# Feed-forward weights staged in other buffers and made ternary in two passes, with new work orders

## What is computed

```python
x = x + tanh(g_xattn) * xattn(layernorm(x), ctx, mask)      # 8 heads of 64
x = x + tanh(g_ffn) * ffn(layernorm(x))                     # 512 -> 2048 -> 512

def act_quant(x):      # per row, 8 bits
    scale = 127.0 / clip(max(abs(x)), 1e-5)
    return clip(round(x * scale), -128, 127) / scale
def weight_quant(w):   # one scale for the whole matrix; values -1, 0, 1
    scale = 1.0 / clip(mean(abs(w)), 1e-5)
    return clip(round(w * scale), -1, 1) / scale
def bitlinear(x, w, b):
    return act_quant(rmsnorm(x)) @ weight_quant(w).T + b
def ffn(x):
    return bitlinear(gelu(bitlinear(x, w1, b1)), w2, b2)
```

## Time and profile before

| | us |
|---|---|
| three runs, lowest / median / highest | 1079.02 / 1079.19 / 1079.51 |
| the profiled execution, its own time | 1082.41 |
| its span, first to last instruction | 1080.6 |
| TensorE busy | 1017.6 (94%) |
| ScalarE busy | 854.5 (79%) |
| VectorE busy | 816.6 (76%) |
| GpSimd busy | 770.4 (71%) |

### The profile page before, as it was taken

How to read it: one execution, slowest core, us unless ns; L and a number is a source line. 1 busy time by engine, 2 the same in 40 slices (tenths; PEclk the granted TensorE clock), 3 DMA queues, 4 the chain that set the end, 5 groups by cost and what they waited for, 6 DMA issues and landing times.

```text
span 1080.6 us, 24141 instructions
## 1 busy us (share of the span) xinstructions
PE 1017.6 (94%) x8516; PEld 599.7 (55%) x8516; DVE 816.6 (76%) x1769; ACT 854.5 (79%) x1465; POOL 770.4 (71%) x743
## 2 busy tenths in 40 slices
PE   2958999999999999999999999999999999999686
...
GB/s 294 165 215 166 187 146 175 134 171 150 167 154 132 170 164 167 150 169 171 141 163 119 167 182 148 163 158 165 140 165 140 166 176 148 166 119 145 142 64 98
DMA packets 480038, 170.79 MB, mean 158 GB/s; under 512 B 458288, under 2 KB 460080, under 8 KB 479536
## 3 DMA queue, kind: packets, MB, share of 16 engines
...
## 4 chain that ended last, share of the span: by engine, by line
PE 81%; ACT 6%; POOL 4%; issue 3%; DVE 3%; DMA 2%; SPq 0%; ACTq 0%; DVEq 0%; POOLq 0%
PE ps_g L602 44%; PE ps_s L632 11%; PE ps_g L706 9%; PE ps_g L659 9%; PE ps_g L695 7%; PE ps_g L647 2%; POOL p L1097 1%; POOL ctx L1108 1%; ACT prob L961 1%; ACT hq L1056 1%; ACT p L968 1%; ACT h_sb L1049 1%; DMA xr<-in_wk 1%; DMA pt<-p 1%; ACT L1049 0%
## 5 line engine op out<-in xcount | busy, mean ns | idle before, releaser
L1097 POOL TENSOR_TENSOR p<-prob,p 112x750 f16<-112x750 f32 x256 | 402.6, 1580 | 118.2 <-ACT p L968 115.4
L782 DVE CUSTOM_DVE_ANT_0 prob<-ps_s,mbias 112x750 f32<-112x750 f32 x256 | 237.0, 936 | 93.3 <-PE ps_s L632 88.8
L602 PE MATMUL ps_g<-ctx,wk 128*128 128x375 f16 x1152 | 203.8, 328 | 34.9 <-POOL ctx L1108 31.2
L961 ACT ACTIVATE prob<-prob,rmin 112x750 f32<-112x750 f32 x256 | 233.0, 913 | 2.0 <-DVE rmin L782 1.6
L602 PE MATMUL ps_g<-wv,ctx 128*128 128x512 f16 (+1 forms) x864 | 199.5, 380 | 0.0
L602 PEld LDWEIGHTS ps_g<-ctx,wk 128*128 128x128 f16 x1152 | 111.2, 99 | 119.5 <-issue 30.0
L632 PE MATMUL ps_s<-k_sb,q_sb 64*112 64x375 f16 x1536 | 150.6, 329 | 7.1 <-DVE rmin L782 6.4
L602 PEld LDWEIGHTS ps_g<-wv,ctx 128*128 128x128 f16 (+1 forms) x864 | 85.1, 103 | 92.6 <-issue 6.3
L968 ACT ACTIVATE p<-prob 112x750 f16<-112x750 f32 x160 | 130.9, 821 | 7.0 <-DMA pt<-p 6.4
L632 PEld LDWEIGHTS ps_s<-k_sb,q_sb 64*112 64x112 f16 x1536 | 89.9, 127 | 63.8 <-issue 39.5
L659 PE MATMUL ps_g<-pt,v_sb 128*64 128x224 f16 (+1 forms) x2448 | 122.8, 255 | 1.5 <-DMA pt<-p 1.5
...
## 6 DMA issues: line engine op xcount, KB each, us to landing
...
pt<-p SPq DMA_TRANSPOSE x256, 4.0
...
```

The costliest lines, as they stand in the source:

```text
L602: mm = nc.tensor.matmul(out, lhs, rhs, start=(m == 0), stop=(m == len(steps) - 1))
L782: nc.vector.tensor_tensor_reduce(prob[:, (b * NU + n) % PROBS, :].rearrange("p (c k) -> p c k", c=2), ps_s[0:HT, n % 2, :, 0:CH], mbias[:, ...
L961: nc.scalar.activation(prob[:, (b * NU + n) % PROBS, :], prob[:, (b * NU + n) % PROBS, :], ACT.Exp, bias=rmin[:, n:n + 1], scale=-1.0, acc ...
L1097: nc.gpsimd.tensor_tensor(p16[:, u % HILO, 1, 0:J], prob[:, (b * NU + n) % PROBS, :], p16[:, u % HILO, 0, 0:J], ALU.subtract).then_inc(s[" ...
```

## The change

All in one file:
- The middle pass WR is gone, with its semaphore and its constant. WB now multiplies by the inverse mean and by 2^-9, in place. WQ cuts the float piece to between -2^-9 and 2^-9 and writes it as fp8, whose smallest step near zero is 2^-9, so that the conversion rounds to -2^-9, 0 or 2^-9. The factor is put right in the scales of the two products (one constant each).
- The pieces of both matrices are staged in w1's room, hq, hqt, xr, h_sb and b1, none in pt or v_sb. WA writes its unneeded output to a new small buffer. The waits of T:0:0 and V:0:1 on the weights go; the loads, LR and BD wait for WQ (w_quant) where they waited for WR.
- WM's first step, the sum over eight columns on VectorE, is a token of its own, WS.
- All five orders are new. The start reaches one batch further (FIRST is 2): pieces 8 to 15 are loaded, scaled and cut along with batch 1, and the first tile's feed-forward stands in the start. The cycle and the end hold the same work in another order.

```diff
-MAGIC = 12582912.0
+W_UNIT = 2.0 ** -9
-FIRST, LAST = 1, 14
+FIRST, LAST = 2, 14
 SP start
-    LX:0:0 PD:0:0 LC:0:0 LC:1:0 LC:2:0 PD:1:0 XT:0:0 LX:0:1 XT:1:0 LM:0:0 PD:2:0 WL:1:0 WL:0:0 WL:2:0 WL:3:0
-    WL:8:0 WL:4:0 WL:5:0 WL:6:0 WL:7:0 PD:3:0 WL:9:0 LC:0:1 LX:0:2 WL:13:0 LC:1:1 LC:2:1 WL:14:0 WL:12:0 WL:10:0
-    T:0:0 WL:11:0 T:1:0 T:2:0 T:3:0 WL:15:0 T:4:0 BD:0:0 T:5:0 XT:0:1 XT:1:1 T:6:0 T:7:0 T:8:0 LC:0:2 LC:1:2
...
+    LC:0:0 LX:0:0 PD:0:0 LC:1:0 LC:2:0 PD:1:0 PD:2:0 XT:0:0 XT:1:0 LM:0:0 WL:0:0 WL:1:0 WL:2:0 LX:0:1 LC:0:1
+    LC:1:1 WL:3:0 WL:4:0 WL:5:0 WL:6:0 WL:7:0 T:0:0 PD:3:0 LC:2:1 LX:0:2 T:1:0 LC:0:2 T:2:0 T:3:0 BD:0:0 XT:0:1
+    XT:1:1 T:4:0 T:5:0 T:6:0 LM:0:1 WL:8:0 WL:9:0 T:7:0 T:8:0 WL:10:0 WL:11:0 T:9:0 T:10:0 T:11:0 LR:1:0 LC:1:2
+    T:12:0 WL:12:0 T:13:0 T:14:0 WL:13:0 T:15:0 T:0:1 WL:14:0 WL:15:0 LC:2:2 XT:0:2 XT:1:2 T:1:1 T:2:1 T:3:1
...
 PE start
-    K:0:0 K:1:0 K:2:0 K:3:0 K:4:0 Q:0:0 Q:1:0 Q:2:0 S:0:0 V:0:0 V:1:0 V:2:0 K:5:0 K:6:0 S:1:0 K:7:0 S:2:0 WM:0:0
-    V:3:0 V:4:0 V:5:0 S:3:0 Q:3:0 K:0:1 K:1:1 S:4:0 V:0:1 V:1:1 S:5:0 V:2:1 V:3:1 S:6:0 WM:1:0 PV:0:0 K:2:1
...
+    K:0:0 K:1:0 K:2:0 K:3:0 K:4:0 Q:0:0 Q:1:0 Q:2:0 S:0:0 V:0:0 V:1:0 V:2:0 S:1:0 K:5:0 K:6:0 K:7:0 V:3:0 V:4:0
+    V:5:0 S:2:0 S:3:0 Q:3:0 WM:0:0 S:4:0 K:0:1 V:0:1 V:1:1 S:5:0 PV:0:0 V:2:1 V:3:1 S:6:0 K:1:1 K:2:1 K:3:1
...
 POOL start
-    N1:0:0 CX:0:0 CX:1:0 CX:2:0 N1:0:1 MB:0:0 L:0:0 L:1:0 WB:0:0 WB:1:0 WB:2:0 WB:3:0 H:2:0 CX:0:1 WB:4:0 WB:5:0
-    WB:6:0 WB:7:0 CX:1:1 CX:2:1 L:2:0 L:3:0 L:4:0 H:5:0 H:7:0 L:5:0 L:6:0 L:7:0 N1:0:2 L:8:0 WB:8:0 WB:9:0
...
+    CX:0:0 N1:0:0 CX:1:0 CX:2:0 MB:0:0 N1:0:1 L:0:0 L:1:0 H:2:0 L:2:0 L:3:0 CX:0:1 CX:1:1 L:4:0 CX:2:1 WB:0:0
+    WB:1:0 WB:2:0 H:5:0 L:5:0 L:6:0 WB:3:0 H:7:0 WB:4:0 N1:0:2 L:7:0 L:8:0 H:10:0 WB:5:0 PL:0:0 L:9:0 L:10:0
...
 PE cycle
-    S:5:0 PV:0:0 V:2:1 V:3:1 K:2:1 K:3:1 S:6:0 PV:1:0 K:4:1 F1:4:-1 F1:5:-1 F1:6:-1 F1:7:-1 S:7:0 V:4:1 F2:0:-1
-    K:5:1 S:0:1 PV:2:0 V:5:1 Q:2:1 S:1:1 K:6:1 K:7:1 S:2:1 F2:1:-1
+    PV:0:0 S:5:0 V:2:1 V:3:1 K:2:1 K:3:1 S:6:0 PV:1:0 K:4:1 F1:4:-1 F1:5:-1 F1:6:-1 F1:7:-1 S:7:0 V:4:1 K:5:1
+    S:0:1 V:5:1 F2:0:-1 PV:2:0 S:1:1 K:6:1 K:7:1 Q:2:1 S:2:1 F2:1:-1
 PE end, its last part
-    S:6:15 S:7:15 PV:3:15 F1:4:14 F1:5:14 F1:6:14 F1:7:14 PV:4:15 O:0:15 PV:5:15 PV:6:15 PV:7:15 O:1:15 F2:0:14
+    S:7:15 PV:2:15 PV:3:15 F1:4:14 F1:5:14 F1:6:14 F1:7:14 PV:4:15 PV:5:15 O:0:15 PV:6:15 PV:7:15 F2:0:14 O:1:15
     F1:0:15 F1:1:15 F1:2:15 F1:3:15 F1:4:15 F1:5:15 F1:6:15 F1:7:15 F2:1:14 F2:0:15 F2:1:15
...
+        rough = sb("rough", [128, WCH], BF16)
...
-        W2_AT = [halves_of_h[0], halves_of_h[1], halves_of_xr[0], halves_of_xr[1]] \
-            + [pt_words[:, n * WCH:(n + 1) * WCH] for n in range(3)] + [v_words[:, KC * D:KC * D + WCH]]
-        W1_AT = [own[0], own[1], halves_of_b1[0], halves_of_b1[1], halves_of_h[0], halves_of_h[1], halves_of_xr[0],
-                 halves_of_xr[1]]
+        in_hq = hq[:, :].bitcast(F32)
+        in_hqt = hqt[:, :, :].rearrange("p k q -> p (k q)").bitcast(F32)
+        W2_AT = [own[0], own[1], in_hq, in_hqt, halves_of_xr[0], halves_of_xr[1], halves_of_h[0], halves_of_h[1]]
+        W1_AT = [halves_of_b1[0], halves_of_b1[1], own[1], in_hq, in_hqt, halves_of_xr[1], halves_of_h[0],
+                 halves_of_h[1]]
         FLOATS = W2_AT + W1_AT
-        COMES_AFTER = {NW + 4: 0, NW + 5: 1, NW + 6: 2, NW + 7: 3}
-        COMES_LAST = (2 * NW - 2, 2 * NW - 1)
-        STAGED_IN = {0: 1, 1: 1, 2: 0, 3: 0, NW + 2: 3, NW + 3: 3}
+        COMES_AFTER = {NW + 2: 1, NW + 3: 2, NW + 4: 3, NW + 5: 5, NW + 6: 6, NW + 7: 7}
+        COMES_LAST = (4, NW + 5)
+        STAGED_IN = {4: 0, 5: 0, 6: 1, 7: 1, NW: 3, NW + 1: 3}
...
                     elif n in COMES_AFTER:
-                        sp.wait_ge(w_above, COMES_AFTER[n] + 1)
+                        sp.wait_ge(w_quant, COMES_AFTER[n] + 1)
...
                     u = b * NU + n
-                    if u == 0:
-                        sp.wait_ge(w_above, NW - 1)
...
                 if kind == "WQ":
-                    dve.wait_ge(w_above, n + 1)
-                    nc.vector.tensor_scalar(piece((w2, w1)[n // NW], n), above[n % 2], 2.0, -1.0, ALU.min, ALU.add,
-                                            saturate=False).then_inc(w_quant, 1)
+                    dve.wait_ge(w_near, n + 1)
+                    if n >= NW:
+                        dve.wait_ge(w_quant, NW + 3 if n >= NW + 4 else 2)
+                    nc.vector.tensor_scalar(piece((w2, w1)[n // NW], n), FLOATS[n], W_UNIT, -W_UNIT, ALU.min,
+                                            ALU.max, saturate=False).then_inc(w_quant, 1)
...
-                if kind == "WR":
-
-                    act.wait_ge(w_near, n + 1)
-                    if n >= 2:
-                        act.wait_ge(w_quant, n - 1)
-                    nc.scalar.activation(above[n % 2], FLOATS[n], ACT.Relu, bias=one_up[:, :]).then_inc(w_above, 1)
-                    return
...
                         act.wait_ge(wready, 3)
-                        act.wait_ge(w_above, NW)
...
-                    nc.gpsimd.tensor_scalar(FLOATS[n], FLOATS[n], winv[:, at:at + 1], MAGIC, ALU.mult, ALU.add)\
+                    nc.gpsimd.tensor_scalar(FLOATS[n], FLOATS[n], winv[:, at:at + 1], W_UNIT, ALU.mult, ALU.mult)\
                         .then_inc(w_near, 1)
```

More of the change, by code:

```diff
@@ new lines @@
+    F1:0:-1 F1:1:-1 F1:2:-1 F1:3:-1 N1:0:2 L3:1:-1 M:10:0 M:11:0 KL:1:1 PA:0:0 GM:0:-1 VL:2:1 G2:0:-1 VL:3:1
+    KL:2:1 KL:3:1 M:12:0 M:13:0 PA:1:0 KL:4:1 F1:4:-1 F1:5:-1 F1:6:-1 F1:7:-1 M:14:0 M:15:0 VL:4:1 GM:1:-1
+    G2:1:-1 M:0:1 M:1:1 XN:0:2 F2:0:-1 KL:5:1 VL:5:1 M:2:1 M:3:1 PA:2:0 M:4:1 XH:0:2 KL:6:1 M:5:1 KL:7:1 F2:1:-1
+    QL:2:1 PA:3:0 XH:1:2
+    """, """
+    M:6:14 QL:3:14 M:7:14 O:0:13 L2:0:13 M:8:14 L3:0:13 M:9:14 O:1:13 L2:1:13 VL:0:15 VL:1:15 KL:0:15 M:10:14
+    PA:0:14 KL:1:15 M:11:14 F1:0:13 F1:1:13 F1:2:13 F1:3:13 M:12:14 M:13:14 KL:2:15 KL:3:15 KL:4:15 L3:1:13
@@ L485, in build @@
         own = [w1[:, n * 4 * WCH:(n + 1) * 4 * WCH].bitcast(F32) for n in range(2)]
-        W2_AT = [halves_of_h[0], halves_of_h[1], halves_of_xr[0], halves_of_xr[1]] \
-            + [pt_words[:, n * WCH:(n + 1) * WCH] for n in range(3)] + [v_words[:, KC * D:KC * D + WCH]]
-        W1_AT = [own[0], own[1], halves_of_b1[0], halves_of_b1[1], halves_of_h[0], halves_of_h[1], halves_of_xr[0],
-                 halves_of_xr[1]]
-        FLOATS = W2_AT + W1_AT
-        COMES_AFTER = {NW + 4: 0, NW + 5: 1, NW + 6: 2, NW + 7: 3}
-        COMES_LAST = (2 * NW - 2, 2 * NW - 1)
-        STAGED_IN = {0: 1, 1: 1, 2: 0, 3: 0, NW + 2: 3, NW + 3: 3}
-        rough = [hqt[:, :, :].rearrange("p k q -> p (k q)").bitcast(BF16)[:, 0:WCH], xc[:, :].bitcast(BF16)]
-        above = [hq[:, :].bitcast(BF16)[:, n * WCH:(n + 1) * WCH] for n in range(2)]
+        in_hq = hq[:, :].bitcast(F32)
[3 more added lines that the diff above has]
+                 halves_of_h[1]]
+        FLOATS = W2_AT + W1_AT
+        COMES_AFTER = {NW + 2: 1, NW + 3: 2, NW + 4: 3, NW + 5: 5, NW + 6: 6, NW + 7: 7}
+        COMES_LAST = (4, NW + 5)
+        STAGED_IN = {4: 0, 5: 0, 6: 1, 7: 1, NW: 3, NW + 1: 3}
         def piece(w, n):
```

175 lines of the change are left out of this document (90 added, 85 removed).

## The result

The kernel after takes 1069.82 us as median of four runs (1066.89 to 1074.12), beside 1079.23 of the kernel before in the same series: 0.9913, interval 0.989 to 0.9937, so 9.4 us less. I had forecast 1060.2, 19 us less. The time lies in the stated range, near its upper end, and half of the forecast gain is missing. The same kernel was run twice more beside the experiments: 0.9922 (0.9907 to 0.9938) and 0.989 (0.9868 to 0.9911). The profiled execution has a span of 1072.3 us and took 1074.12, the longest of its four; against the span of before the gain to be explained is 8.3 us.

The account below looks back on a forecast made before the run. TensorE's own pace bounds the twelve batches, so time comes only from the ends. The start's 17.3 us, taken as 15, plus 4 at the end make 19: 1060.2 us off the median. Forecast 1056 to 1067, stated range 1051 to 1071.

Parts of the forecast that it names:

- First context: At the very start, the first context piece goes first, so the first matmul starts at 15.8 instead of 19.55: 3.7 us gained.
- Knot and waits: At 57 to 69 us, context ahead of weight pieces gains 5.8 us; shorter waits for q and attention low halves gain 3.8.
- Clock: In the start, TensorE's slow stretches after 69.29, 102.72 and 124.25 us all go: 4.0 us gained.
- Third pass: Weight rounding in the start: 18.2 us of ScalarE work goes, VectorE's clamping takes 1.9 us each; off the path.
- WL:15's cover: Near 100 us, this weight load holds up a context load, but batch 2's context has 10 us of cover.
- Twelve cycles: In the twelve batch cycles, the same products in another order: counted as zero.
- The 2 us of cover: In each cycle, turned hidden values take 10.3 us while TensorE has 12.3 us of other work: 2 us to spare.
- the twelvefold rival: Two transposes late in every cycle, the excess paid twelve times; slower, 1092 at 2.7 us excess; chance 0.06.
- The end: After the cycles, shorter row-minimum waits and earlier norm and quantization of tile 25: 4 us gained, bounds 0 and 8.
- row-minimum waits: At the end, two waits totalling 6.0 us shrink to about 2.0 each: gain 2.
- the slow run of 16 products: At the end, tile 25's feed-forward ran slow, 6.46 us, after waiting for turned input; its norm now comes before.
- VectorE as the bound of the start: Clamping passes all at 3.38 us add 32 us in the start and take back its gain: 1075 to 1079; chance 0.06.

Follow-up runs that it names:

- ctx_first: The kernel before with only the first context piece loaded, copied and split ahead of x and W_k; 1076.6 us, 0.9956.
- start_back: The kernel after with the start of the kernel before, keeping the new cycle and end; 1081.23 us, 1.0011.
- third_back: The kernel after with a ScalarE copy of each scaled weight piece added, for which VectorE's clamping waits; 1075.65 us, 0.996.
- knot_only: The kernel before with batch 1's context pieces moved ahead of weight pieces, keeping three passes and all buffers; 1081.9 us, 1.0.
- cycle_back: The kernel after with the cycle of the kernel before, keeping the new start and end; 1068.3 us, 0.9893.
- start_only: The kernel before with the start of the kernel after, keeping the old cycle and end; 1068.16 us, 0.989.

## Why half of the forecast gain is missing

- **First context, 3.7 forecast.** 4.0 in the profile (19.55 to 15.53), 4.4 in time by ctx_first. Right, and it passed through whole.
- **Knot and waits, 5.8 and 3.8 forecast.** From the first matmul to the first feed-forward product the waits sum to 19.2 us before (the earlier trace rows less the first, and two of 0.6 and 0.4) and 9.5 after: 9.7 against 9.6 (6.1 and 8.3 in the two repeats). The sum was right in this execution, its parts weren't: the context wait vanished altogether, q still cost 2.7, turned scores 1.9.
- **Clock, 4.0 forecast.** This step failed. I had counted all slow stretches as gone "since no wait after the first exceeds 3.1 us". None does, but behind the waits of 1.9, 1.9 and 2.7 stand products that take about 3.0, 1.6 and 1.4 us more than at full clock (51 to 58, 101 to 106, 120 to 123 us): 6.0. Before had 5.0 and not 4.0: the prediction left out twelve products at 104.69 us that take 2.45 us where the same take 1.32 elsewhere. For the same 914 products of the start TensorE is busy 114.6 us before and 115.5 after, so the term is minus 0.9 instead of 4.0, 4.9 us off, and the largest error of this execution. 4.0 + 9.7 - 0.9 is the 12.8 measured. In the two repeats the term is minus 1.2 and plus 2.3, under 4.0 in each. Before's own start was busy only 112.2 us in start_back's profile, so one pair of profiles gives this term to some 2 us.
- **Third pass, off the path.** The clamping pass has a mean of 1.2 us against 1.9 forecast, and the 16 keep VectorE busy 19.0 us where before had 22.4. But third_back says that ScalarE's pass was worth about 5 us: the prediction that it lies off the path was wrong. Whether ScalarE's load or the extra handover counts isn't shown. I had the gain in the knot's row without giving it its cause; knot_only shows that the order of GpSimd, ScalarE and SP alone doesn't bring it.
- **Behind 140 us.** I had no term here. Of the 3.0 us lost from there to 228 us, 2.6 are waits: one of 1.5 and four of about 0.3 us, where before has one of 0.17. The repeats lose 2.7 and 2.4. The largest wait is behind the centering passes that GpSimd's run holds. WL:15's cover held: no wait for a context half stands after the first.
- **Twelve cycles, 0 forecast.** Minus 1.9 over ten of the twelve, minus 1.1 and 0.9 in the repeats. Three small waits make 1.1 us of it where before has 0.2; the rest isn't placed. The waits for turned hidden values (0.34 there, 0.41 at 914 us) come in single batches and not in each. The 2 us of cover were about right; the twelvefold rival was wrong.
- **The end, 4 forecast.** 0.4 in this execution, 2.5 and 4.1 in the repeats against the same profile of before. But the old end alone takes 212.1 to 216.1 us in four profiles, so single profiles don't settle this term. By the times it isn't 4: with the same start and cycle, the new end gives 1068.3 us (cycle_back) and the old one 1068.16 (start_only), though the intervals leave 3 us either way. The row-minimum waits fell from 6.0 to 4.9, not to 4, and the last wait from 6.85 to 4.5. Against it the slow run of 16 products, which I had counted as gone, only moved: 6.44 us at 1045.15 behind a wait of 3.7 for the last tile's turned input. The waits for turned scores grew too, from 1.5 to 4.1. In all TensorE waits 19.4 us there where before has 20.3. Moving work from one wait to the next is no gain where each wait leaves a slow stretch.
- **VectorE as the bound of the start** (third rival). Named for the clamping passes, and they were harmless. The mechanism, sharing with GpSimd, was the right one and struck a one-column product and the centering passes.

Of the 10.7 us between the forecast's 19 and the 8.3 of the span, 4.9 are the clock, 3.0 the time behind 140 us, 1.9 the cycles and 3.6 the end. That is 13.4. Against it stand 0.4 us gained beyond the terms and the 2.3 by which I had taken the start's 17.3 down to 15. This is the account of one execution, the slowest of its four. What all three profiles share is the clock term under 4.0, the 2.4 to 3.0 us lost behind 140 us and the 0.9 to 1.9 in the cycles.
